# Routing stage of a two-layer kernel: four buffers of each kind, work of the next group written ahead, stores issued by the sync engine

## What is computed

```python
def _layernorm(x, axis=-1, eps=1e-05):
    m = jnp.mean(x, axis=axis, keepdims=True)
    v = jnp.var(x, axis=axis, keepdims=True)
    return (x - m) / jnp.sqrt(v + eps)
...
    x = L0_attn_hidden_states                # (16, 1024, 256)
    xn = _layernorm(x, axis=-1)
    s = _L0_attn_ref(xn, ...)
    g = _silu(_L0_ffn_ref(xn, L0_ffn_router_w, ...))
    x = x + s * g
...
        scores = jax.nn.softmax(jnp.einsum('bsd,ed->bse', x, router_w), axis=-1)
```

## Time and profile before

| | us |
|---|---|
| median of 3 runs | 4614.92 |
| lowest and highest run | 4613.5, 4615.97 |
| span of the profiled execution | 4612.0 |
| first transposes of the routing stage start | 12.0 |
| its last products end | 244.4 |
| DMA issues of the next stage start | 257.4 |
| routing stage by group (232 us over 32) | 7.25 |

### The profile page before, as it was taken

One profiled execution on the slowest core, in us unless ns is written; L12 is line 12 of the kernel. 1 busy time (PEld: TensorE's weight loads), 2 busy tenths in 40 slices (PEclk: granted clock), 3 DMA queues, 4 the chain that ended last, 5 costly groups with the idle time before them and its releaser, 6 DMA issues. The chain is left out here.

```text
span 4612.0 us, 79916 instructions
## 1 busy us (share of the span) xinstructions
PE 4189.6 (91%) x28828; PEld 3314.9 (72%) x28828; DVE 2751.5 (60%) x5151; ACT 1976.9 (43%) x3701; POOL 1694.4 (37%) x1338
## 2 busy tenths in 40 slices
PE   6759999999999999799999999999995989999985
PEld 6636555555555556698888989898995878777774
DVE  4447777777767777334343433434433688888886
ACT  2214444444444444444454444445442444444441
POOL 1123333333333333344444444444432233333333
PEclk9999999999999999899999999999997999999998
DMA  6611011011011010223223232323224334444433
GB/s 205 214 44 38 29 38 34 29 38 34 29 38 34 29 38 29 81 42 64 48 56 60 41 66 43 62 47 59 42 40 92 93 98 111 105 95 111 101 61 41
DMA packets 254043, 294.80 MB, mean 64 GB/s; under 512 B 21600, under 2 KB 226656, under 8 KB 251616
## 3 DMA queue, kind: packets, MB, share of 16 engines
q0 software_dynamic: 88064, 117.74, 15.2%
q1 hardware_dynamic: 140000, 138.26, 9.3%
q10 hardware_dynamic: 25600, 33.56, 2.2%
HBM read 155.15 MB, written 134.35 MB: 63 GB/s over the span
## 5 line engine op out<-in xcount | busy, mean ns | idle before, releaser
L523 DVE TENSOR_TENSOR e_hTl<-e_hf,e_hTh 128x512 fp32r<-128x512 f32 x512 | 355.0, 693 | 795.4 <-ACT e_hTh L465 795.4
L1018 POOL TENSOR_TENSOR a_mix<-a_tmp,a_h 128x512 f32<-128x512 f32 x320 | 393.9, 1251 | 808.4 <-DVE a_tmp L1105 651.9
L384 POOL DMA_INDIRECT acc_d<-e_y,e_sids x256 | 402.0, 1570 | 715.6 <-DVE e_y L539 670.8
L464 ACT ACTIVATE e_hf<-ps_heads,e_b 128x512 f32<-128x512 f32 x512 | 355.3, 694 | 697.8 <-PE ps_heads L611 690.6
L611 PE MATMUL ps<-e_w2h,e_hTh 128*128 128x256 f32 x2048 | 580.1, 283 | 0.0
L611 PE MATMUL ps<-e_w2h,e_hTl 128*128 128x256 f32 x2048 | 576.5, 281 | 0.0
L611 PE MATMUL ps<-e_w2l,e_hTh 128*128 128x256 f32 x2048 | 571.3, 279 | 0.0
L611 PE MATMUL ps_heads<-e_xTh,e_w1h 128*128 128x512 f32 x1024 | 419.4, 410 | 26.8 <-issue 22.8
L611 PE MATMUL ps_heads<-e_xTh,e_w1l 128*128 128x512 f32 x1024 | 407.6, 398 | 0.0
L611 PE MATMUL ps_heads<-e_xTl,e_w1h 128*128 128x512 f32 x1024 | 407.2, 398 | 0.4 <-issue 0.3
L611 PEld LDWEIGHTS ps<-e_w2h,e_hTh 128*128 128x128 f32 x2048 | 385.0, 188 | 19.8
(11 more groups left out here) (294 smaller groups left out, 9458.6 us busy)
## 6 DMA issues: line engine op xcount, KB each, us to landing
r_x<-in_L_attn_hidden_states SPq DMA_DIRECT2D x32, 512.0 KB, 4.6
xn_d<-r_xn ACTq DMA_DIRECT2D x32, 512.0 KB, 3.1
xnT_d<-r_xT ACTq DMA_DIRECT2D x32, 512.0 KB, 3.6
acc_d<-a_zeros POOLq DMA_DIRECT2D x32, 512.0 KB, 3.0
s_d<-a_s SPq DMA_DIRECT2D x32, 512.0 KB, 2.8
e_w<-in_L_ffn_w SPq DMA_DIRECT2D x16, 1024.0 KB, 4.8
f_a<-acc_d SPq DMA_DIRECT2D x32, 512.0 KB, 3.8
f_x<-s_d SPq DMA_DIRECT2D x32, 512.0 KB, 5.2
```

Source lines behind the costliest of these rows:

```text
L384: pool.indirect_dma_start(acc_d, bass.IndirectOffsetOnAxis(ap=sids[:, GT * q + t:GT * q + t + 1], axis=0), ys[r][:, t, :], None, compute_o ...
L464: nc.scalar.activation(hf[m % 2][:], ps[2 + m % 2][:], ACT.Gelu, bias=b1s[:, m:m + 1])
L523: nc.vector.tensor_tensor(hT[q % 2][1][:, m, :], hf[m % 2][:], hT[q % 2][0][:, m, :].bitcast(F32), ALU.subtract).then_inc(h_sb, 1)
L1018: nc.gpsimd.tensor_tensor(mix[n][:, m, :].rearrange("p (c t) -> p c t", c=GT), tmp[i % 2][:].rearrange("p (c t) -> p c t", c=GT), h[q % 2] ...
```

## The change

All of it is in `route_phase`; the other stages are unchanged, but their lines stand 36 further down.

- **Buffers.** `r_x`, `r_xn` and `r_xT` become rings of four (`RING`), `r_stats`, `r_mv`, `r_vare` and `r_rstd` have two each. PSUM is used as before.
- **DVE.** The statistics of group g+1 are written ahead of the normalisation of group g. The waits for the store of `r_xn` and for the transposes now concern group g-4 and stand ahead of the normalisation.
- **PE.** The transposes of group g are written ahead of the products of group g-1.
- **ACT.** It issues no DMA. Its copies of `r_xT` of group g stand ahead of the copy of the logits of g-1.
- **SP.** It issues all loads and all stores. For each group: wait for the normalisation of g, store `r_xn` of g, load `r_x` of g+4; wait for ACT's copies of g-1, store `r_xT` of g-1. At the start the load of group 0 stands ahead of that of the router's weights, and the loads of groups 1 to 3 follow.
- **Loops.** Each engine's program has four groups written out, a loop of six turns of four groups, and four groups written out (`each_group`), where it was one loop of sixteen turns of two groups. The starting counts of semaphores (`sem_inc`) fall away.

```diff
-        xg = [sb(f"r_x{r}", [P, GT, D]) for r in range(2)]
-        xn = [sb(f"r_xn{r}", [P, GT, D]) for r in range(2)]
-        xT = [sb(f"r_xT{r}", [P, KD, GN]) for r in range(2)]
+        RING = 4
+        xg = [sb(f"r_x{r}", [P, GT, D]) for r in range(RING)]
+        xn = [sb(f"r_xn{r}", [P, GT, D]) for r in range(RING)]
+        xT = [sb(f"r_xT{r}", [P, KD, GN]) for r in range(RING)]
...
+        def each_group(eng, one):
+
+            for r in range(RING):
+                one(0, r, True, False)
+            with eng.Fori(1, NG // RING - 1) as i:
+                for r in range(RING):
+                    one(i, r, False, False)
+            for r in range(RING):
+                one(NG // RING - 1, r, False, True)
...
         def _(sp):
...
+            def one(i, r, first, last):
+                g = RING * i + r
+                sp.wait_ge(normed, g + 1)
+                sp.dma_start(xn_v[:, bass.ds(GT * g, GT), :], xn[r][:]).then_inc(xn_out[r], 16)
+                if not last:
+                    load(g + RING, r)
+                if not first or r:
+                    store_turned(g - 1, (r - 1) % RING)
+
+            load(0, 0)
             sp.dma_start(wr[:], router_w).then_inc(w_in, 16)
...
         def _(dve):
...
+            def one(i, r, first, last):
+                g, v = RING * i + r, r % 2
+                if not last or r < RING - 1:
+                    statistics(i, r + 1)
+                dve.wait_ge(rstd_ready, g + 1)
+                if not first:
+
+                    dve.wait_ge(xn_out[r], 16 * i)
+                    dve.wait_ge(turned, g - RING + 1)
+                for t in range(GT):
+                    done = nc.vector.tensor_scalar(xn[r][:, t, :], xg[r][:, t, :], mv[v][:, t, 0:1], rstd[v][:, t:t + 1],
+                                                   ALU.subtract, ALU.mult)
+                done.then_inc(normed, 1)
...
         def _(act):
...
+            def one(i, r, first, last):
+                g = RING * i + r
+                act.wait_ge(turned, g + 1)
+                if not first:
+
+                    act.wait_ge(xT_out[r], 16 * i)
+                    act.wait_ge(routed, g - RING + 1)
+                for k in range(KD):
+                    nc.scalar.copy(xT[r][:, k, :], ps[2 * (r % 2) + k][:]).then_inc(xT_sb, 1)
+                if not first or r:
+                    logits(g - 1, (r - 1) % RING)
...
         def _(pe):
...
+            def one(i, r, first, last):
+                g = RING * i + r
+                pe.wait_ge(normed, g + 1)
+                if not first or r >= 2:
+                    pe.wait_ge(xT_sb, 2 * g - 2)
+                for k in range(KD):
                     for t in range(GT):
...
+                done.then_inc(turned, 1)
+                if not first or r:
+                    route(g - 1, (r - 1) % RING, first and r <= 2)
```

More of the change, by code:

```diff
@@ L146, in _ @@
             pool.wait_ge(zeroed, 1)
-            with pool.Fori(0, NG) as it:
-                pool.wait_ge(var_ready, it + 1)
-                nc.gpsimd.tensor_tensor(rstd[:], vare[:], power[:], ALU.pow).then_inc(rstd_ready, 1)
+            with pool.Fori(0, NG // 2) as i:
+                for r in range(2):
+                    pool.wait_ge(var_ready, 2 * i + r + 1)
+                    nc.gpsimd.tensor_tensor(rstd[r][:], vare[r][:], power[:], ALU.pow).then_inc(rstd_ready, 1)
         @block.vector
@@ L152, in _ @@
         def _(dve):
[L153 to L177, removed]
@@ new lines, in statistics @@
+            def statistics(i, r):
+                i, r = (i + r // RING, r % RING)
+                g, v = RING * i + r, r % 2
+                dve.wait_ge(x_in[r], 16 * i + 16)
+                for t in range(GT):
+                    done = nc.vector.bn_stats(out=stats[v][:, t, :], in_=xg[r][:, t, :])
+                done.then_inc(stats_o, 1)
+                dve.wait_ge(stats_o, 2 * g + 1)
+                dve.sem_inc(spare, 1)
+                for t in range(GT):
+                    done = nc.vector.bn_aggr(out=mv[v][:, t, :], in_=stats[v][:, t, :])
+                done.then_inc(stats_o, 1)
+                dve.wait_ge(stats_o, 2 * g + 2)
+                nc.vector.tensor_scalar(vare[v][:], mv[v][:, :, 1], EPS, None, ALU.add).then_inc(var_ready, 1)
@@ L198, in _, with logits @@
         def _(act):
[L199 to L220, removed]
+            def logits(g, r):
+                act.wait_ge(routed, g + 1)
+                nc.scalar.copy(logit[:, bass.ds(GT * g, GT), :],
+                               ps[4 + r % 2][:, 0:GT * NE].rearrange("p (t e) -> p t e", t=GT)).then_inc(logit_sb, 1)
@@ new lines, in route @@
+            def route(g, r, begin):
+                pe.wait_ge(xT_sb, 2 * g + 2)
+                if not begin:
+                    pe.wait_ge(logit_sb, g - 1)
+                for t in range(GT):
+                    for k in range(KD):
+                        done = nc.tensor.matmul(ps[4 + r % 2][:, t * NE:(t + 1) * NE], xT[r][:, k, t * P:(t + 1) * P],
+                                                wr[:, k, :], start=(k == 0), stop=(k == KD - 1))
+                done.then_inc(routed, 1)
```

65 lines of the change are left out of this document (31 added, 34 removed).

## The result

| | before | after |
|---|---|---|
| median, us | 4615.44 (4 runs, 4613.5 to 4621.8) | 4543.15 (4 runs, 4540.25 to 4547.06) |
| ratio | | 0.9844, 95% interval 0.983 to 0.9858 |
| span of the profiled execution | 4612.0 | 4545.4 |
| last products of the stage end | 244.40 | 174.90 |
| next stage's first DMA issue | 257.4 | 187.6 |

Sixty-nine and a half of the 72 us are gone when the stage ends (244.40 - 174.90).

The account below looks back on a forecast made before the run. The routing stage was taken as bound by transposes, copies, products (7.25 us a group), afterwards by PE at 5.19. Products ending at 180.1 for 244.4 us gave -64, less 2: 4614.9 - 62 = 4553 us, range 4546 to 4572.

Parts of the forecast that it names:

- PE becomes the bound: Routing stage: PE works without a gap at 5.19 us a group, copies hidden; 4546 to 4560 us, chance 0.77.
- The size of PE's group: Routing stage on PE: eight transposes at 0.219 us plus sixteen product records at 0.215 us make 5.19 us a group.
- Two us for a ragged start and the back edges: Routing stage: 2 us taken off the gain for loads and stores sharing the queue at the start and five back edges.
- Five us for another placement of the code: Later stages, same code shifted: 5 us allowed either way, as PE's back-edge stall in the experts' loop varies.
- Transfers: Routing stage's loads and stores on one queue: 4.3 to 5.1 us a group, just under PE's 5.19.
- DVE waiting for `r_x`: Routing stage: with PE idle time ended by the normalisation, the sign that transfers are the bound.
- The lower end of that rival: Routing stage's transfers as bound, up to 5.83 us a group: 4553 + 7, so 4560 us; chance 0.12.
- DVE's waits for the transposes of four groups before: Routing stage: a sign that the prediction is right, DVE's waits turning to waits for these PE transposes.
- Code missed in the larger loop: PE's routing loop of about 200 records misses its code: five back edges cost 27 us, 4580 us; chance 0.04.
- Copies in the chain: Routing stage: a wait ties products of g-1 to copies of g; 6.54 us a group, 4592 us; chance 0.03.
- One transfer at a time: Routing stage's single queue: each transfer waits for the one ahead, 11.3 us a group, 4745 us; chance 0.02.
- Transfers bound: Routing stage: three transfers a group on one queue cost up to 5.83 us, 4560 to 4573 us; chance 0.12.

Follow-up runs that it names:

- pe_order_back: The kernel after with PE's order alone undone, so a group's products stand right behind its transposes again: 4591.32 us, ratio 0.9952.
- before_pe_ahead: The kernel before with PE's order alone changed, transposes of g+1 ahead of products of g, two buffers kept: 4610.04 us, ratio 0.9986.
- pad_20: The kernel after with 10 unused transposes (20 instructions) more on PE behind the last routing products: 4557.23 us, ratio 0.9874.
- pad_60: The kernel after with 30 unused transposes (60 instructions) more on PE behind the last routing products: 4519.3 us, ratio 0.9796.
- half_products: The kernel after with only the first half of the depth multiplied in the routing products, logits wrong: 4478.88 us, ratio 0.97.
- two_buffers: The kernel after with rings of two in place of four and one more block of two groups written out: 4676.25 us, one run.

## Why the prediction was wrong, point by point

- **PE becomes the bound: right.** Its idle time in mid-stage is zero, and the copies, the table, DVE and SP are hidden, as forecast. Taking back DVE's order or the stores, which the prediction costed at nothing, changed nothing.
- **The size of PE's group: the step that failed.** The prediction multiplied sixteen product records by a spacing of 0.215 us, 3.44 us. They cost 3.27, and 32 x 0.17 = 5.4 us. The 3.44 was right for the block that I read it from: 3.43 us from 110.20 to 113.63 in before, and 3.44 in pe_order_back. Both follow an idle wait for the copies. In after the products follow transposes without a gap, and the whole difference lies at their start: taken one by one, the second product record starts 0.07 us after the first in after and 0.235 in all 32 groups of before, and from there on they are 0.213 apart in both. The step that failed is that I took the cost of a block behind a wait for its cost behind busy work. No row of the routing stage before has such products without a wait ahead, so this could not be read there. Why the first record costs less is open.
- **Two us for a ragged start and the back edges: not there,** a second and smaller miss of the same sum. First and second transposes start at 12.67 and 15.91, for 12.0 and 15.6, and from there PE never waits. With the 5.4 us, less the later start, that makes up the 7.2 us by which the stage ends sooner than the 182 us of the sum.
- **The rest, 2.6 us of the 9.8** by which the forecast of 4552.9 was too high, is no larger than what the profiled executions leave open. Their spans differ by 66.6 us, less than the 69.5 of the stage; but the profiled run of after was the slowest of its four, 3.9 us over their median, and that of before the fastest of its four, 1.9 under. The later stages are as long as before within 3 us or so (the recurrence 1541.8 us for 1542.7).
- **Five us for another placement of the code: right here, by luck.** The code grew by 499 instructions, nearly twice 256, and the second stop moved by 13 instructions only. The term was far too small: other places of the code made the recurrence 27 us shorter (before_pe_ahead) and the whole kernel 16 us slower or 22 faster (pad_20, pad_60).
- **Transfers:** I put them at 4.3 to 5.1 us a group, just under PE. They can do 4.0. My sign for them, DVE waiting for `r_x`, appeared (31.8 us) without their being the bound. A wait is a sign only if PE waits behind it. The lower end of that rival, 7 us over the sum, came from no row. DVE's waits for the transposes of four groups before, which I forecast, did not show.
- **Rivals.** Code missed in the larger loop: refuted, the back edge of 210 PE records a turn takes 0.208 us (median). Copies in the chain: refuted, PE never waits for them. One transfer at a time: refuted by 318 GB/s. Transfers bound: refuted by half_products.

```profile
L136 PEldq COMPARE_BRANCH  x6: 76/208/243, 47.4 to 147.7; - x6
```

## What to carry to other kernels

A block's cost belongs to what stands ahead of it: sixteen product records took 3.44 us behind a wait and 3.27 behind busy work. When a change removes the wait, take the cost from a place in the trace where the block follows the neighbour that it will have, or allow for the difference. An order that runs ahead and the buffers for it are one change: the order without the buffers lost 63 us (two_buffers), PE's part of it alone made the stage 25 us longer (before_pe_ahead), and the buffers without PE's order won nothing beyond the table (pe_order_back). So follow each queue that the moved work holds back. Before believing a gain or loss of half a per cent on a kernel with large loops, compare an untouched stage in both traces, and look for idle time marked "issue" behind the loops' branches: sixty instructions of padding in a place where the engine waits anyway took 22 us off this kernel, and twenty cost 16.

## What the hardware showed that I had not expected

- Behind a branch back over a long loop PE can stop a second time, 12 to 53 instructions later, for 0.8 to 3.6 us, by where the code stands modulo 256 instructions. The granted clock behind such a pair of stops was 0.77 over 15 us, for 1.00 behind a single one (first return of the recurrence's loop).
- Sixteen records of small fp32 products took 3.27 us behind transposes without a gap and 3.44 behind a wait; only the first spacing differs (0.07 and 0.235 us).
- A DMA share of 0.98 at 318 GB/s was no limit: the same queue held 392 GB/s over 80 us, at a share of 1.08.
- ACT's table was loaded in every turn of a loop (16 times 1283 ns) when the loop held the engine's first such instruction, and once when one stood ahead of it.
